# Contextual attention and a gated convolution on one core: the Gram matrix of the patches in fp32 on 64x64 tiles instead of three fp16 products

## What is computed

```python
x = x + contextual_attention(gn(x), mask)
x = x + conv(gn(x), build_weight(weight, alphas, betas)) + bias
# contextual_attention(f, mask), for every image:
fd = f[:, :, ::2, ::2]                                  # 64 channels, 8 x 8 pixels, L = 64
w = extract_patches(fd, 3, 1, pad=1)                    # L patches of 64 x 3 x 3
norm = sqrt(sum(w * w, axis=(2, 3, 4), keepdims=True))
yi = einsum('npckl,nqckl->nqp', w, w / max(norm, 1e-4)) # the Gram matrix, L x L, rows scaled
yi = fuse(fuse(yi, 3) with rows and columns turned, 3)  # two sums of three diagonals
yi = softmax(yi * mm * 10, axis=1) * mm
out = deconv(yi, 4 x 4 patches of f) / 4
```

## Time and profile before

| | before |
|---|---|
| median of 3 runs | 55.9 us (55.76 to 56.01) |
| profiled execution, span from first to last instruction | 53.4 us |
| what the median has beyond that span | 2.5 us |
| PE, PEld busy | 39.2, 25.6 us |
| DVE, ACT, POOL busy | 34.8, 16.0, 19.5 us |
| chain that ended last | DVE 42%, PE 30%, DMA 6%, issue 3%, ACT 3% of the span |
| matmuls of `gram` (L488) | 108 records, 4.2 us busy |

### The profile page before, as it was taken

The page is one execution under the profiler, slowest core; times in us unless marked ns, Lnnn a source line. Parts: engine busy times, 40 slices in busy tenths (PEclk is TensorE's granted clock), DMA queues, the critical chain, the costliest instruction groups (busy, mean ns, idle before and its releaser), DMA issues.

```text
span 53.4 us, 1316 instructions
## 1 busy us (share of the span) xinstructions
PE 39.2 (73%) x502; PEld 25.6 (48%) x502; DVE 34.8 (65%) x143; ACT 16.0 (30%) x50; POOL 19.5 (37%) x49
## 2 busy tenths in 40 slices
PE   1996757996999988999589908999999999000000
PEld 0331242673389876986369704444468886000000
DVE  3907799769896889999999999959990200300000
ACT  4500304666752352726798420004300000000000
POOL 5994887979999600203006960000000000000000
PEclk9999999999999999999999999999999999999555
DMA  0399996000000000000000000000000111111110
GB/s 0 88 370 228 310 184 140 5 0 0 18 0 0 0 0 0 12 0 0 0 12 0 0 0 0 0 0 0 0 0 18 37 42 48 49 48 49 48 49 18
DMA packets 2335, 2.37 MB, mean 44 GB/s; under 512 B 281, under 2 KB 2201, under 8 KB 2330
## 3 DMA queue, kind: packets, MB, share of 16 engines
q1 hardware_dynamic: 1770, 1.96, 14.3%
q10 hardware_dynamic: 560, 0.33, 2.0%
HBM read 1.77 MB, written 0.52 MB: 43 GB/s over the span
## 4 chain that ended last, share of the span: by engine, by line
DVE 42%; PE 30%; DMA 6%; issue 3%; ACT 3%; DVEq 0%
PE bank L583 12%; PE bank L595 12%; DMA xh<-x_in_dram 6%; DVE gn_stats L674 4%; DVE wrec L761 3%; PE bank L488 3%; DVE x2h L704 2%; DVE fst L704 2%; DVE ftl L822 2%; DVE pst L807 2%; DVE x L830 2%; DVE xn L704 2%; DVE n2c L774 2%; DVE p L807 1%; DVE gn_mv L678 1%
## 5 line engine op out<-in xcount | busy, mean ns | idle before, releaser
L478 PE MATMUL bank<-idle 128*128 128x512 f16 x27 | 8.7, 455 | 1.1 <-POOL idle L278 1.1
L305 POOL TENSOR_SCALAR fq<-xh,gn_mean,gn_rstd 128x128 f32<-128x128 f32 x8 | 6.7, 852 | 0.2 <-DVE xn L704 0.2
L488 PE MATMUL bank<-fmv,fst 128*64 128x128 f16 x108 | 4.2, 224 | 1.0 <-ACT fmv L381 0.8
L921 DVE SCALAR_TENSOR_TENSOR o_sb<-bank,x1b 128x256 f32<-128x256 f32 x4 | 1.6, 422 | 5.0 <-PE bank L595 5.0
L543 PE MATMUL bank<-k_sb,pst 128*64 128x256 f16 (+2 forms) x72 | 4.3, 262 | 0.8 <-DVE pst L713 0.7
L488 PEld LDWEIGHTS bank<-fmv,fst 128*64 128x64 f16 x108 | 3.3, 108 | 2.8 <-ACT fmv L381 2.8
L478 PEld LDWEIGHTS bank<-idle 128*128 128x128 f16 x27 | 2.7, 116 | 4.2 <-issue 1.8
L337 POOL TENSOR_TENSOR wl<-w,wh 64x288 f16<-64x288 f32 x4 | 2.9, 726 | 3.6 <-ACT wh L457 3.4
L543 PEld LDWEIGHTS bank<-k_sb,pst 128*64 128x64 f16 x72 | 3.3, 109 | 1.5 <-DVE pst L713 0.8
L360 ACT ACTIVATE gn_ln<-gn_var 128x2 f32<-128x2 f32 x4 | 0.8, 204 | 9.6 <-DVE gn_var L687 9.5
L583 PE MATMUL bank<-x2h,wh 128*128 128x512 f16 x9 | 2.4, 388 | 1.6 <-DVE x2h L704 1.6
(11 more groups left out here) (120 smaller groups left out, 90.7 us busy)
## 6 DMA issues: line engine op xcount, KB each, us to landing
xg<-x_in_dram SPq DMA_DIRECT2D x2, 256.0 KB, 6.2
out_dram<-o_sb SPq DMA_DIRECT2D x4, 128.0 KB
k_sb<-k_dram SPq DMA_DIRECT2D x1, 496.0 KB, 5.8
xh<-x_in_dram SPq DMA_DIRECT2D x1, 256.0 KB, 3.2
xh<-x_in_dram ACTq DMA_DIRECT2D x1, 256.0 KB, 3.6
w_sb<-weight_in_dram SPq DMA_DIRECT2D x1, 72.0 KB, 2.9
c_sb<-c_dram ACTq DMA_DIRECT2D x1, 64.0 KB, 3.0
c_sb<-c_dram SPq DMA_DIRECT2D x1, 64.0 KB, 5.9
```

Of the source, the lines that this page charges most:

```text
L305: pool.tensor_scalar(fq[u][:, j, 2 * q:2 * q + 2, :].rearrange("p s (a b) -> p s a b", a=G), xh[u][:, j, :].rearrange("p (a r b s) -> p r ...
L478: te.matmul(ps, idle[:, 0:P], idle[:, :], start=True, stop=True)
L488: i = te.matmul(gram_ps[u][half(g), :, :], st, mv[:, :, k // 3:k // 3 + G, k % 3:k % 3 + G], start=part_st == part_mv == k == 0, stop=part ...
```

## The change

f is kept in fp32. `fst` is one fp32 tile per unit with the three shifts, without a low part; `fmv` and `xn` are gone, and with them the copies into `fmv` on DVE and ACT, the subtraction and the second set of shifts. `gram` multiplies fp32 slices of `fst` with themselves: for each of 9 taps, 2 h and 2 g one matmul of 64 partitions, 64 weight columns and 64 moving columns, in the order centre, right and left copy, each with its own semaphore. The images h = 0 and 1 go into different banks (u and u + 4). Both units' Gram matrices are complete before `fuse1` of unit 0. `normalise_gram` is four tensor_scalar per unit instead of two tensor_tensor. The fills are 5 before unit 0's f and 4 before unit 1's. POOL's `f_by_parity` is released by the centre of f instead of xn.

```diff
-FILL = {"x": 8, "statistics": 4, "high f of unit 0": 5, "low f of unit 0": 1, "high f of unit 1": 4,
-        "low f of unit 1": 3, "sums of unit 0": 2}
+FILL = {"x": 8, "statistics": 4, "f of unit 0": 5, "f of unit 1": 4, "sums of unit 0": 2}
...
-        xn = per_unit("xn", P, IPU, L)
-
-        fst = per_unit("fst", P, 3, 2 * IPU, (G + 2) * G, dt=fp16)
-        fmv = per_unit("fmv", P, 2 * IPU, 2, (G + 2) ** 2, dt=fp16)
+        fst = per_unit("fst", P, 3, IPU, (G + 2) * G)
...
-        gram_ps = [bank[u][:, 0:IPU * L].rearrange("p (i s) -> p i s", i=IPU) for u in u2]
-        y2_ps = gram_ps
+        gram_ps = [[bank[u + 4 * h][:, 0:L] for h in range(2)] for u in u2]
+        y2_ps = [bank[u][:, 0:IPU * L].rearrange("p (i s) -> p i s", i=IPU) for u in u2]
...
-            pool.wait_ge(xn_ready, 1)
+            pool.wait_ge(f_center, 1)
             f_by_parity(0, 0)
...
-            def copies_of_f(u, part):
-                act.wait_ge((fh_center, fl_center)[part], u + 1)
-                shift_right(fst[u], part).then_inc(f_copied[u][part], 1)
-                act.activation(inner(fmv[u][half(1), of(part), 1, :]), rows(fst[u][half(1), 1, of(part), G:G + L]),
-                               ACT.Copy).then_inc(f_copied[u][part], 1)
+            def right_of_f(u):
+                act.wait_ge(f_center, u + 1)
+                shift_right(fst[u], 0).then_inc(f_right, 1)
...
-            act.wait_ge(zeros_f, 2 * UNITS)
+            act.wait_ge(zeros_f, UNITS)
             gn_seed(0, 0)
-            copies_of_f(0, 0)
-            copies_of_f(0, 1)
+            right_of_f(0)
             gn_seed(0, 1)
...
-            copies_of_f(1, 0)
+            right_of_f(1)
             norm_seed(0)
-            copies_of_f(1, 1)
...
-            def gram(u, parts):
-
-                for part_st, part_mv in parts:
-                    te.wait_ge(f_copied[u][max(part_st, part_mv)], 4)
-                    for k in range(TAPS):
-                        for g in range(2):
-                            st = fst[u][:, k % 3, IPU * part_st + g, G * (k // 3):G * (k // 3) + L]
-                            mv = fmv[u][:, IPU * part_mv + g, :, :].rearrange("p h (a b) -> p h a b", b=G + 2)
-                            i = te.matmul(gram_ps[u][half(g), :, :], st,
-                                          mv[:, :, k // 3:k // 3 + G, k % 3:k % 3 + G],
-                                          start=part_st == part_mv == k == 0, stop=part_st == 1 and k == TAPS - 1)
+            def gram(u):
+
+                for n, dj in enumerate((1, 2, 0)):
+                    te.wait_ge((f_right, f_center, f_left)[dj], u + 1)
+                    for di in range(3):
+                        for h in range(2):
+                            for g in range(2):
+                                f = fst[u][half(h), dj, g, G * di:G * di + L]
+                                i = te.matmul(gram_ps[u][h][half(g), :], f, f, start=n == di == 0,
+                                              stop=n == 2 and di == 2)
                 return i
...
-            keep_clock(FILL["high f of unit 0"], bank[4][:, :])
-            gram(0, ((0, 0),))
-            keep_clock(FILL["low f of unit 0"], bank[6][:, :])
-            gram(0, ((0, 1), (1, 0))).then_inc(gram_done, 1)
-            keep_clock(FILL["high f of unit 1"], bank[6][:, :])
-            gram(1, ((0, 0),))
-            keep_clock(FILL["low f of unit 1"], bank[6][:, :])
-            gram(1, ((0, 1),))
+            keep_clock(FILL["f of unit 0"], bank[4][:, :])
+            gram(0).then_inc(gram_done, 1)
+            keep_clock(FILL["f of unit 1"], bank[6][:, :])
+            gram(1).then_inc(gram_done, 1)
             te.wait_ge(k_in, 16)
             fuse1(0, 0)
...
-            gram(1, ((1, 0),)).then_inc(gram_done, 1)
...
-            for t in fst + fmv:
+            for t in fst:
                 dve.memset(flat(t).bitcast(fp32), 0.0).then_inc(zeros_f, 1)
...
+            def full_f(u):
 
                 gn_rstd(0, u)
                 for j in range(IPU):
-                    i = normalise(rows(fst[u][:, 1, 0:IPU, G:G + L])[:, j], even(u, j), norm[0][u], j)
-                i.then_inc(fh_center, 1)
-                copies_of_f(u, 0)
+                    i = normalise(rows(fst[u][:, 1, :, G:G + L])[:, j], even(u, j), norm[0][u], j)
+                i.then_inc(f_center, 1)
+                dve.wait_ge(f_center, u + 1)
+                shift_left(fst[u], 0).then_inc(f_left, 1)
...
             gn_moments(0, 1, xh[1])
-            high_f(0)
             full_f(0)
-            low_f(0)
             gn_var(0, 1, GN_EPS)
-            high_f(1)
+            full_f(1)
...
-                r = rnorm[u][:, :].rearrange("p (i s) -> p i s", s=1).broadcast_to([P, IPU, L])
-                dve.tensor_tensor(yh[u][:, :, 1:L + 1], gram_ps[u], r, ALU.mult).then_inc(yh_ready, 1)
-                dve.tensor_tensor(y32[u][:, :, :], gram_ps[u], r, ALU.mult).then_inc(y32_ready, 1)
+                for dst, done in ((yh[u][:, :, 1:L + 1], yh_ready), (y32[u][:, :, :], y32_ready)):
+                    for j in range(IPU):
+                        i = dve.tensor_scalar(dst[:, j, :], gram_ps[u][j], rnorm[u][:, j:j + 1], None, ALU.mult)
+                    i.then_inc(done, 1)
...
             norms(0)
-            full_f(1)
-            low_f(1)
             inverse_norms(0)
             normalise_gram(0)
```

More of the change, by code:

```diff
@@ L195, in build @@
             "moments", "groups", "var_ready", "mean_ready", "gn_y0"))
-        xn_ready, fh_center, fl_center, fq_ready = map(sem, ("xn_ready", "fh_center", "fl_center", "fq_ready"))
-        f_copied = [[sem(f"f_copied{u}{part}") for part in range(2)] for u in range(UNITS)]
+        f_center, f_left, f_right, fq_ready = map(sem, ("f_center", "f_left", "f_right", "fq_ready"))
         gram_done, n2_ready, norm_y0, y32_ready, yh_ready, yl_ready = map(sem, (
@@ L226, in of @@
             return slice(IPU * part, IPU * part + IPU)
-        def inner(ap):
-            side = G + 2
-            return ap.rearrange("p i (a b) -> p i a b", b=side)[:, :, 1:side - 1, 1:side - 1]
         u2 = range(UNITS)
-        gram_ps = [bank[u][:, 0:IPU * L].rearrange("p (i s) -> p i s", i=IPU) for u in u2]
-        y2_ps = gram_ps
+        gram_ps = [[bank[u + 4 * h][:, 0:L] for h in range(2)] for u in u2]
+        y2_ps = [bank[u][:, 0:IPU * L].rearrange("p (i s) -> p i s", i=IPU) for u in u2]
         y1_ps = [bank[2 + u][:, 0:IPU * (G + 2) * G].rearrange("p (i s) -> p i s", i=IPU) for u in u2]
@@ L318, in _ @@
             f_by_parity(0, 1)
-            pool.wait_ge(xn_ready, 2)
+            pool.wait_ge(f_center, 2)
             for j in range(IPU):
@@ L714, in shift_left @@
                                        rows(t[:, 1, of(part), G:G + L])[:, :, :, 1:G])
-            def copies_of_f(u, part):
-                dve.wait_ge((fh_center, fl_center)[part], u + 1)
-                shift_left(fst[u], part).then_inc(f_copied[u][part], 1)
-                dve.tensor_copy(inner(fmv[u][half(0), of(part), 0, :]),
-                                rows(fst[u][half(0), 1, of(part), G:G + L])).then_inc(f_copied[u][part], 1)
-            def high_f(u):
+            def full_f(u):
                 gn_rstd(0, u)
                 for j in range(IPU):
-                    i = normalise(rows(fst[u][:, 1, 0:IPU, G:G + L])[:, j], even(u, j), norm[0][u], j)
-                i.then_inc(fh_center, 1)
-                copies_of_f(u, 0)
-            def full_f(u):
-                for j in range(IPU):
-                    i = normalise(xn[u][:, j, :].rearrange("p (a b) -> p a b", a=G), even(u, j), norm[0][u], j)
-                i.then_inc(xn_ready, 1)
-            def low_f(u):
-                dve.wait_ge(xn_ready, u + 1)
-                dve.tensor_tensor(fst[u][:, 1, of(1), G:G + L], xn[u][:, :, :], fst[u][:, 1, of(0), G:G + L],
-                                  ALU.subtract).then_inc(fl_center, 1)
-                copies_of_f(u, 1)
-            dve.wait_ge(zeros_f, 2 * UNITS)
+                    i = normalise(rows(fst[u][:, 1, :, G:G + L])[:, j], even(u, j), norm[0][u], j)
+                i.then_inc(f_center, 1)
+                dve.wait_ge(f_center, u + 1)
+                shift_left(fst[u], 0).then_inc(f_left, 1)
+            dve.wait_ge(zeros_f, UNITS)
             dve.wait_ge(x_in[0], 16)
@@ L769, in norms @@
                 for j in range(IPU):
-                    i = dve.scalar_tensor_tensor(gdiag[u][:, j, :], gram_ps[u][:, j, :], 1.0,
+                    i = dve.scalar_tensor_tensor(gdiag[u][:, j, :], gram_ps[u][j], 1.0,
                                                  k_sb[:, K_DIAG:K_DIAG + L], ALU.mult, ALU.mult,
```

## The result

| | before | after |
|---|---|---|
| median of 4 runs each, on one chip | 55.83 us (55.73 to 56.01) | 55.03 us (54.87 to 55.39) |
| ratio to before | 1 | 0.987 [0.983, 0.991] |
| profiled execution, span | 53.4 us | 52.7 us (the execution: 54.87) |

The account below looks back on a forecast made before the run. It took PE's Grams to set fuse1's start, with DVE's chain following: −1.7 (norms(1)) − 0.45 (stall) + 0.1 (normalise_gram) = −2.0, from 55.9 to 53.9 us; own range 53.5 to 54.4, 8 in 10 from 53.4 to 57.3.

Parts of the forecast that it names:

- The Gram on PE, the term that decides: fp32 Gram on PE: 36 matmul pairs a unit at 58 ns each, 2.1 us a unit.
- rival (1): Gram on PE: weight loads become the bound, a pair keeps 110 ns, Gram 4.0 us, time 57.6; chance 0.22.
- (2): Gram on PE takes 2.35 to 3.1 us and n2c falls under the memsets: 55.4 to 55.9; chance 0.13.
- PE sets the time: Start of fuse1 of unit 0: set by PE's Grams, 13.6 instead of 15.16; norms(1) then 1.7 us earlier.
- rival (4): Faster Gram on PE, 35 to 50 ns a pair: yh then binds from 13.15, time 53.4; chance 0.07.
- in PE's shadow: Unit 0's normalise_gram: its extra 0.1 us lies hidden behind PE's work, in a shadow 0.45 us wide.
- A stall of DVE: n2c in norms(1) on DVE: issued before POOL's memsets, so not held, 0.17 instead of 0.64; saves 0.45 us.
- normalise_gram +0.1: Scaling the Gram on DVE: four tensor_scalar take 0.63 instead of 0.52, costing 0.1 us in unit 1.
- The sum: All terms up to the kernel's end: −1.7 − 0.45 + 0.1 = −2.0 us.
- Rival (3): DVE's Newton steps are held by POOL's memsets until 17.65: time 55.0; chance 0.15.
- Rival (5): The clock falls to 1.2 GHz in a gap of PE; slower, chance 0.03 together with any other cause.
- the statistics 1.2 earlier: Unit 1's statistics on DVE (gn_dif): start at 8.7 instead of 9.89, 1.2 us earlier.

Follow-up runs that it names:

- e9: Kernel after with unit 1's Gram computed twice in a row, the second over the first: 55.14 us, ratio 0.987.
- e8: e2 with POOL's first fq held until unit 1's left copy of f is made: 54.83 us, ratio 0.982.
- e4: Kernel after with 8 instead of 4 fills on PE behind unit 0's statistics: 55.19 us, ratio 0.988.
- e2: Kernel after with POOL's memsets of x2h and x2l moved to its start, ahead of the mask: 54.64 us, ratio 0.980.
- e5: Kernel before with POOL's memsets of x2h and x2l moved to its start: 55.56 us against 55.92, ratio 0.993.
- e7: Kernel after with the edits of e2, e3 and e4 together: 54.63 us, ratio 0.975.
- e3: Kernel after with normalise_gram's four tensor_scalar per unit replaced by four tensor_tensor with a broadcast operand: 54.54 us, ratio 0.978.
- e12: e10 with four more fills on PE ahead of fuse1 of unit 0: 54.43 us, ratio 0.972.
- e1: Kernel after run again with no edit: 55.07 us, ratio 0.985.
- e10: Kernel after with the edits of e3 and e4, and POOL's x2 memsets moved behind its first share of the weights: 54.23 us, ratio 0.972.
- e11: e10 with POOL's first fq also held until unit 1's left copy of f, as in e8: 54.44 us, ratio 0.971.

## Why the prediction was wrong

**"The Gram on PE, the term that decides" failed.** 58 ns a pair was taken from transpose_f and put_x, which work with one tile, or with tiles that take all rows. In the trace of after, 72 records last 1.28 us, of which the last record is 0.22; its 18 steps of four records (two pairs each) start 59 ns apart, all but the first. That is 29 ns a pair, half of the forecast's; with the last record the unit takes what the forecast had as its lower bound, 1.3. The 58 ns was the right time for a *step*, but a step holds two pairs. The rows of two weight loads that start together spoke for it; the forecast used them against rival (1) and not on its own term. The rivals (1) and (2) fall with it. By e9 the error has no part in the time, though: PE had 0.85 to spare, and the forecast's 2.1 is only 0.82 above 1.28, so a Gram at the forecast's price would have cost nothing either.

**"PE sets the time" failed, from the other side.** This is the step that decided. PE has 0.85 to spare (e9), and DVE binds. That was rival (4), but with yh written from 12.8 and ready at 13.15, which gave 53.4. It was written from 13.45, 0.65 later. The parts: f of unit 1 0.19 late (gn_ya beside fq took 0.32), its copy 0.36 instead of 0.25, norms(0) waiting 0.18 for a Gram at 1.2 GHz, and nya with 0.27 instead of 0.14: 0.61 together. e8 shows fq's part, 0.36 up to norms(0), and e4 the clock's, 0.3. The two overlap and can't be added. Then normalise's extra 0.27 in unit 0, which was to lie "in PE's shadow", came on top. So norms(1) was at 16.20 and not 15.4.

**"A stall of DVE": right in cause, wrong in outcome.** It is POOL's memsets that hold n2c, as e2 and e5 show. But by the traces n2c is held wherever it meets them, so it had to be over before they begin at 16.14, and norms(1) had to start by 15.57 (0.40 to n2c and its 0.17); it was at 16.20. That is worked out, and no run has n2c so early. The forecast treated the two terms as a sum; they are tied, and the second is lost with a part of the first. With both in hand (e7), fq took 0.24 of it. The Trainium skill, "SBUF — State Buffer", section "Who interferes with whom", says that a DVE tensor_scalar in one of the modes that use the port pair shared with GpSimd is blocked for the whole of a GpSimd instruction that was issued first. The traces agree that n2c is held, and go further: with 1.04 and 1.10 us it outlasts the ends of three memsets of 0.36 and comes free after the fourth.

**"normalise_gram +0.1" was mis-sized:** 0.38 a unit, of which e3 gives 0.25 to the form with a scalar for each partition; the other 0.13 is four instructions in place of two, which the forecast had at 0.1.

**The sum:** 0.8 (norms(1)) + 0.37 (the stall) + 0.27 (normalise) = 1.4 of the −2.0 were not there, which leaves −0.6; −0.67 was seen at the last eviction, −0.7 in the span and −0.8 in the medians. The 2.5 us that the forecast added to its span were too much as well: the other executions of before have 2.1 to 2.2 beyond theirs (53.4 at 55.59, 53.9 at 56.04), so the profiled one was a short one, and the forecast's span of 51.4 stood for some 53.6.

**Rival (3)** gave 55.0, which is the time measured, but not by its mechanism: nya of unit 1 came behind the memsets, at 17.64, and in e12 a DVE instruction with two SBUF inputs was not held under them. A Newton step itself never lay under them. **Rival (5)** was given too little: the clock does fall early, in some executions. Its price is 0.3 at norms(0), which the wall hides, 0.4 under the transposes (e1), and 1.7 where it lasts twice as long (e10).

**What held:** the statistics 1.2 earlier, the memsets' start to 0.2, and that everything behind norms(1) moves one to one.

## What to carry to other kernels

When a change takes work from one engine, price the second chain as finely as the first: here PE stood waiting 0.4 us for yh, and what decided were short vector instructions, each one or two tenths dearer than priced. Before two gains are added, ask whether the second needs the first; a block of instructions that holds another engine is a wall with a date, and a gain ahead of it can be lost in the wait for it (e4), so move the block first if nobody is waiting for it. Work that only bridges a wait stands in the queue like any other, and a slow clock can make it the longest thing there (e11). And a row priced for one tile says nothing of several tiles side by side until a row with several is found.

## What the hardware showed that was not expected

- Four 64x64 tiles in fp32 take 59 ns a step at 2.4 GHz for 64 loaded and 64 streamed columns each, two pairs; the four weight loads, 0.13 long each, start within 20 ns. At 1.2 GHz it is 107 ns a step. The order of the tiles moves a unit only from 1.28 to 1.45 us.
- A tensor_scalar of 64 columns from PSUM with a scalar for each partition follows its like after 0.20 us; with a constant, or as a tensor_tensor with a broadcast operand, after 0.13.
- A two-element DVE tensor_scalar was held up to 1.10 us by four memsets in a row, and ended 0.02 to 0.03 after the end of the third or the fourth. An fp16 copy was held too (0.42 instead of 0.20, e12), an instruction with two SBUF inputs wasn't (0.48 with and without).
- Eight fills took 3.57 us in one execution and 1.89 in others at a recorded clock of 1.00 in both (e11, e12).
- The granted clock fell to 0.50 from 7.85 to 11.26 in one execution of the kernel after and from 16.20 to 19.60 in another, with the same instructions; PE was busy through either stretch. Ahead of the first, from 5.0 to 7.8 us, it was busy for 1.80 us, and for 2.62 in e4, where the clock stayed full. Why it falls at one place or the other stays open.
